# Feed-forward stage: rotation cosines read from PSUM, GELU table load moved, q/k norm by halves, order of the last DVE steps changed

## The reference

```python
h = shift_token(x)
q, k, v = split(h @ wqkv, 3)                    # 8 heads of 64
q, k = l2norm(q) * qs, l2norm(k) * ksc
q, k = rotary_xpos(q, k)                        # q*cos*scale + rotate_half(q)*sin*scale
o = local_attention(q, k, v)                    # band of 64, softmax
x = x + o @ wo
h = layernorm(shift_token(x)) * lg + lb
a, g = split(h @ w1 + b1, 2)
x = x + (a * gelu(g)) @ w2 + b2
```

## Time and profile before

| | |
|---|---|
| three executions | 2468.91, 2474.99, 2475.39 us; median 2474.99 |
| profiled execution | 2465.03 us, span 2462.9 us |
| mean granted clock of TensorE | 0.946 of full speed |
| busy: PE, DVE, ACT, POOL | 2116.9, 1809.3, 1462.6, 1058.3 us |

### The profile page before, as it was taken

One profiled execution on the slowest core, in us unless ns is written; L12 is line 12 of the kernel. 1 busy time (PEld: TensorE's weight loads), 2 busy tenths in 40 slices (PEclk: granted clock), 3 DMA queues, 4 the chain that ended last, 5 costly groups with the idle time before them and its releaser, 6 DMA issues. The chain is left out here.

```text
span 2462.9 us, 56322 instructions
## 1 busy us (share of the span) xinstructions
PE 2116.9 (86%) x23398; PEld 1565.7 (64%) x23398; DVE 1809.3 (73%) x2815; ACT 1462.6 (59%) x2389; POOL 1058.3 (43%) x800
## 2 busy tenths in 40 slices
PE   2799999998989868999868999999989997597968
PEld 1566666666666645555536667676666664495758
DVE  3688888888888646777727888888888884563556
ACT  0477776766666515666546776766666674363635
POOL 4665555545555210000035565655555450550245
PEclk8799999999999968999979999999999998698979
DMA  7000000079999995000000000000000003121122
GB/s 151 1 2 1 2 2 2 1 78 105 111 137 129 126 127 51 2 2 2 2 1 1 2 2 2 2 2 2 2 2 2 1 2 76 54 66 37 35 75 80
DMA packets 211376, 90.91 MB, mean 37 GB/s; under 512 B 79700, under 2 KB 206721, under 8 KB 210996
## 3 DMA queue, kind: packets, MB, share of 16 engines
q1 hardware_dynamic: 202596, 72.27, 24.5%
q0 software_dynamic: 6080, 11.76, 1.5%
q10 hardware_dynamic: 2448, 3.28, 0.6%
HBM read 24.31 MB, written 63.41 MB: 36 GB/s over the span
## 5 line engine op out<-in xcount | busy, mean ns | idle before, releaser
L490 POOL TENSOR_TENSOR work<-work,rot_tables 128x512 f32<-128x512 f32 x256 | 382.6, 1515 | 317.3 <-ACT work L594 317.3
L498 POOL TENSOR_TENSOR work<-work 128x1024 f32<-128x1024 f32 x128 | 304.8, 2381 | 283.6 <-DVE work L924 278.4
L941 DVE TENSOR_TENSOR work<-work,small 128x1024 f32<-128x1024 f32 x128 | 234.4, 1833 | 56.6 <-ACT small L608 50.1
L924 DVE TENSOR_TENSOR work<-work,rot_tables 128x1024 f32<-128x1024 f32 x128 | 219.3, 1713 | 11.6 <-ACT work L594 11.6
L1081 DVE TENSOR_REDUCE small<-psum 128x4 f32<-128x1024 f32 x128 | 156.6, 1223 | 90.3 <-PE psum L1582 88.5
L1482 PE MATMUL psum<-centered,ffn_w 128*128 128x256 f32 x768 | 191.2, 401 | 3.0 <-DVE centered L985 2.9
L705 ACT ACTIVATE work<-psum 128x1024 f32<-128x1024 f32 x128 | 131.0, 1024 | 88.7 <-PE psum L1582 88.4
L1323 PE MATMUL psum<-qkv_w_hi,h_hi 128*128 128x512 f32 x384 | 180.0, 469 | 2.2 <-ACT work L594 2.2
L1420 PE MATMUL psum<-work 64*128 64x128 f32 (+1 forms) x2048 | 178.9, 304 | 0.0
L1482 PEld LDWEIGHTS psum<-centered,ffn_w 128*128 128x128 f32 x768 | 146.0, 197 | 31.2 <-DVE centered L985 4.4
L1453 PE MATMUL psum<-work,v 128*32 128x192 f32 (+1 forms) x4096 | 164.8, 302 | 0.0
(11 more groups left out here) (279 smaller groups left out, 5266.1 us busy)
## 6 DMA issues: line engine op xcount, KB each, us to landing
h_area<-mean_weights SPq DMA_DIRECT2D x24, 2048.0 KB
tile_x<-h_area SPq DMA_DIRECT2D x39, 128.5 KB, 2.1
stage<-in_consts ACTq DMA_DIRECT2D x1, 2817.0 KB, 12.0
tile_x<-h_area SPq DMA_DIRECT2D x39, 64.5 KB, 1.8
work<-in_x SPq DMA_DIRECT2D x4, 512.0 KB, 27.2
expert_w<-in_ew SPq DMA_DIRECT2D x1, 2048.0 KB, 8.4
expert_w<-in_ew SPq DMA_DIRECT2D x8, 256.0 KB, 6.6
work<-y_tokens SPq DMA_DIRECT2D x4, 512.0 KB, 6.1
```

What stands on the lines that cost most here:

```text
L490: last = pool.tensor_tensor(b[:, :, :, o_], a[:, :, :, i_], tab[:, l, 1, t, :, o_].unsqueeze(2).to_broadcast([P, 2, HEADS, 32]), ALU.mult)
L498: pool.tensor_tensor(rC[:, t, :], rC[:, t, :], rB[:, t, :], ALU.add).then_inc(f_sum, 1)
L924: dve.tensor_tensor(g(rC[:, t, :]), g(rA[:, t, :]), tab[:, l, 0, t, :, :].unsqueeze(2).to_broadcast([P, 2, HEADS, DH]), ALU.mult)\
L941: dve.tensor_tensor(c_, c_, sm[0][:, 96 + 16 * t:112 + 16 * t].unsqueeze(2).to_broadcast([P, 16, DH]), ALU.mult).then_inc(f_nrm, 1)
```

## The change

- `cosines(i, t)` reads q and k from PSUM instead of from the SBUF copy, as soon as `qk(i, t)` is done. `copy_qk(i, t)` on ACT now waits until `cosines(i, t)` has read them.
- On DVE `cosines(i, 0)` moves up, ahead of `resid`, and `cosines(i, 1)` takes its old place.
- In `scores` the wait for `copy_qk(i, 0)` moves from the front to the third group of masks.
- On ACT the GELU table is asked for after `rstd`; `copy_v` comes ahead of `copy_qk(i, 1)`.
- `clip` and `rnorm` are done for each half t by itself. `rnorm(i, 0)` comes behind `gelu`, `rnorm(i, 1)` after two of the three `exps` and after `x_square`.
- On DVE the end of the turn becomes `gated`, `qk_norm(i, 0)`, `x_center`, `sums(i, 1)`, `clip(i, 1)`, `qk_norm(i, 1)`, `o_norm(i-1, 0)`, `resid2`. Before, it is `gated`, `sums(i, 1)`, `clip`, `x_center`, `qk_norm(i, 0)`, `resid2`, `qk_norm(i, 1)`, `o_norm(i-1, 0)`.
- `rotated` on POOL is two instructions of half the length. In `qk_T` all transposes of k come ahead of those of q. On PE `x_var` goes behind `attend(i-1, 1)`.

```diff
 MASKED = -1e30
 LN_SET = "natural_log_exp_and_others"
+GELU_SET = "gelu_and_others"
 
 
...
                     pool.wait_ge(f_sin, 2 * i + t + 1)
                     pool.wait_ge(f_cos, 2 * i + t + 1)
-                    pool.tensor_tensor(rC[:, t, :], rC[:, t, :], rB[:, t, :], ALU.add).then_inc(f_sum, 1)
+                    for h in range(2):
+                        n_ = slice(h * INNER, (h + 1) * INNER)
+                        last = pool.tensor_tensor(rC[:, t, n_], rC[:, t, n_], rB[:, t, n_], ALU.add)
+                    last.then_inc(f_sum, 1)
 
                 def normed(s):
...
             def ffn(f):
                 def copy_qk(i, t):
-                    act.wait_ge(f_qk, 3 * i + t + 1)
-                    free(act, f_cos, 2 * i + t - 1)
+                    act.wait_ge(f_cos, 2 * i + t + 1)
                     free(act, f_sin, 2 * i + t - 1)
                     src = PS[:, 1 + t:3 + t, :]
...
                     act.activation(V[i % 2][:, :, :], PS[:, 5:7, :], ACT.Copy).then_inc(f_vsb, 1)
 
-                def rnorm(i):
-                    act.wait_ge(f_ssm, i + 1)
-                    link(act.activation(sm[0][:, 64:96], sm[0][:, 32:64], ACT.Ln, scale=65536.0))
-                    act.activation(sm[0][:, 96:128], sm[0][:, 64:96], ACT.Exp, scale=-0.5, bias=half_ln[:, 0:1])\
-                        .then_inc(f_rn, 1)
+                def rnorm(i, t):
+                    part_ = lambda a: sm[0][:, a + 16 * t:a + 16 * t + 16]
+                    act.wait_ge(f_ssm, 2 * i + t + 1)
+                    link(act.activation(part_(64), part_(32), ACT.Ln, scale=65536.0))
+                    act.activation(part_(96), part_(64), ACT.Exp, scale=-0.5, bias=half_ln[:, 0:1]).then_inc(f_rn, 1)
 
                 def copy_q(i):
...
                         square(i - 2)
                         rstd(i - 2)
+                        act.preload_act_table_set(GELU_SET)
                     if new:
+                        copy_v(i)
                         copy_qk(i, 1)
-                        copy_v(i)
                         square_qk(i, 1)
                     if old:
                         gelu(i - 2)
+                    if new:
+                        rnorm(i, 0)
+                    if mid:
+                        exps(i - 1, 0)
+                        exps(i - 1, 1)
                     if pre:
                         x_square(n)
                     if new:
-                        rnorm(i)
+                        rnorm(i, 1)
                     if mid:
-                        for q in range(3):
-                            exps(i - 1, q)
+                        exps(i - 1, 2)
                     if mid:
                         recips(i - 1, 0)
...
                     l, _ = layer_of(i)
                     g = lambda x: x.rearrange("p (g h d) -> p g h d", g=2, h=HEADS)
-                    dve.wait_ge(f_cp, 2 * i + t + 1)
+                    dve.wait_ge(f_qk, 3 * i + t + 1)
                     free(dve, f_qT, i)
-                    dve.tensor_tensor(g(rC[:, t, :]), g(rA[:, t, :]),
+                    dve.tensor_tensor(g(rC[:, t, :]), PS[:, 1 + t:3 + t, :].rearrange("p g (h d) -> p g h d", h=HEADS),
                                       tab[:, l, 0, t, :, :].unsqueeze(2).to_broadcast([P, 2, HEADS, DH]), ALU.mult)\
                         .then_inc(f_cos, 1)
...
                 def sums(i, t):
                     dve.wait_ge(f_sq, 2 * i + t + 1)
-                    dve.tensor_reduce(sm[0][:, 16 * t:16 * t + 16], sq[:, t, :].rearrange("p (g d) -> p g d", d=DH), AX,
+                    dve.tensor_reduce(sm[0][:, 144 + 32 * t:176 + 32 * t:2], sq[:, t, :].rearrange("p (g d) -> p g d", d=DH), AX,
                                       ALU.add).then_inc(f_ss, 1)
 
-                def clip(i):
-                    dve.wait_ge(f_ss, 2 * i + 2)
-                    dve.tensor_scalar(sm[0][:, 32:64], sm[0][:, 0:32], 1e-24, None, ALU.max).then_inc(f_ssm, 1)
+                def clip(i, t):
+                    dve.wait_ge(f_ss, 2 * i + t + 1)
+                    dve.tensor_scalar(sm[0][:, 32 + 16 * t:48 + 16 * t], sm[0][:, 144 + 32 * t:176 + 32 * t:2], 1e-24, None, ALU.max)\
+                        .then_inc(f_ssm, 1)
 
                 def qk_norm(i, t):
-                    dve.wait_ge(f_rn, i + 1)
+                    dve.wait_ge(f_rn, 2 * i + t + 1)
                     dve.wait_ge(f_sum, 2 * i + t + 1)
                     c_ = rC[:, t, :].rearrange("p (g d) -> p g d", d=DH)
...
                     if mid:
                         k_out(i - 1)
+                    if new:
+                        cosines(i, 0)
                     if old:
                         resid(i - 2)
...
                         y_normed(i - 2)
                     if new:
-                        cosines(i, 0)
+                        cosines(i, 1)
                     if mid:
                         m_out(i - 1)
                     if new:
                         sums(i, 0)
-                        cosines(i, 1)
+                        clip(i, 0)
                     if old:
                         gated(i - 2)
                     if new:
-                        sums(i, 1)
-                        clip(i)
+                        qk_norm(i, 0)
                     if pre:
                         x_center(n)
                     if new:
-                        qk_norm(i, 0)
-                    if old:
-                        resid2(i - 2)
-                    if new:
+                        sums(i, 1)
+                        clip(i, 1)
                         qk_norm(i, 1)
                     if mid:
                         o_norm(i - 1, 0)
+                    if old:
+                        resid2(i - 2)
 
             def attn():
...
                         pe.wait_ge(f_nrm, 2 * i + t + 1)
                         last = turned(5, t, INNER)
-                        if t == TILES - 1:
-                            last.then_inc(f_kT, 1)
-                        else:
-                            free(pe, f_on, 2 * i - 1)
+                    last.then_inc(f_kT, 1)
+                    free(pe, f_on, 2 * i - 1)
+                    for t in range(TILES):
                         last = turned(3, t, 0)
                     last.then_inc(f_qT, 1)
...
                     pe.wait_ge(f_kb, i + 1)
                     pe.wait_ge(f_qsb, i + 1)
-                    pe.wait_ge(f_cp, min(2 * i + 3, 2 * ITEMS * (f + 1)))
                     groups = (((3, 6), range(8), P, 0, 0, ms0), ((4, 5), range(4), J0W, 1, WIN, ms1),
                               ((0, 1), range(4, 8), J0W, 1, WIN, ms1))
                     for bs, hs, w, _, _, m in groups:
+                        if bs[0] == 0:
+                            pe.wait_ge(f_cp, min(2 * i + 3, 2 * ITEMS * (f + 1)))
                         bands(bs, len(hs) // 2, w, m)
                     for bs, hs, w, t, k0, _ in groups:
...
                     if mid:
                         attend(i - 1, 0)
+                    if mid:
+                        attend(i - 1, 1)
                     if pre:
                         x_var(n)
-                    if mid:
-                        attend(i - 1, 1)
 
             def attn():
```

## The result

The changed kernel takes 2578.6 us (median of 4, 2572.9 to 2580.7). The kernel before beside it takes 2472.0 (4 runs). The ratio is 1.0436, 95% interval 1.0416 to 1.0456: slower by 107 us, where 93 were forecast. Its profiled execution has a span of 2576.0.

What follows compares the result with a forecast made beforehand. No engine was full, so a chain through several engines was taken to set the pace. Per call 12 x 2.5 + 4 x 0.85 + 14 x 0.8 = 44.6, plus 2; two calls 93; 2475 + 93 = 2568 us, range 2500 to 2620.

Steps and rivals of the forecast that it cites:

- The products wait for the copy: On PE, all products stand behind masks waiting for copy_qk, itself behind cosines; 0.7 us per turn without pre.
- slack before GELU: Earlier rotated(i, 0) may hold m_split and y_normed up to 0.4 per turn, counted as nothing; 24 us without slack.
- S: The start of the first s_max, from which the forecast counts the steps of a turn in us.
- The third `exps` behind `rnorm(i, 1)`: On ACT, the third exps queues behind the later rnorm(i, 1), so attend(i-1, 1) starts at 15.95, not 15.5; 0.1 per turn.
- DVE behind it: DVE's steps from exps through cosines(i+1, 0) fit ahead of resid, possible at 22.25 against 22.16; next s_max at 24.0.
- The turns with a layer 1 item: Feed-forward turns with a layer 1 old item, 14 per call, go from 24.09 to 24.9, +0.8.
- `qk_norm(i, 0)` held by POOL: On DVE, qk_norm(i, 0) could start at 11.3 but ends at 13.15, 1.1 after POOL's rotated; 12.5 if not held.
- The turns with `pre`: Late x_center delays down, and x_rstd delays recips on ACT; 12 turns per call go from 24.24 to 26.7, +2.5.
- Rival (2): Only the terms without pre are real, as x_rstd ends inside attend's time; +50, 2525 us; chance 0.17.
- rival (3): Losses of turns with pre and gains of the others cancel; 2470 to 2480 us; chance 0.04.
- the rival of two more: On ACT, square_qk needs its own table set, adding two loads per turn; +154 on top of 93, 2722 us; chance 0.05.
- Rival (1): Faster: DVE's own list sets the pace and the added waits are covered; 2343 us, or 2410; chance 0.10.

Runs made afterwards that it cites:

- c1b_cos: Kernel before with only the PSUM cosines, their new DVE places, copy_qk waiting for them and copy_v ahead of copy_qk(i, 1); scores wait at the front; ratio 1.0182.
- e1_masks: Changed kernel with the products of the first two groups ahead of the wait for the copy and the third group's masks; ratio 1.0343 to the kernel before.
- e4_sums: Changed kernel with sums and clip of both halves ahead of gated, and rnorm of both ahead of all exps; ratio 1.0244 to the kernel before.
- e5b_xvar_resid2: Changed kernel with x_var back between the two attends and resid2 back ahead of qk_norm(i, 1); ratio 1.0124 to the kernel before.
- e3_xcenter: Changed kernel with x_center back ahead of qk_norm(i, 0); ratio 1.0342 to the kernel before.
- e2_xvar: Changed kernel with x_var back between the two halves of attend; ratio 1.0395 to the kernel before.
- e6b_masks_pool: e1_masks with one more wait on POOL, meant to keep rotated(i, 0) from starting before m_split; ratio 1.0360 to the kernel before.
- g1b_gelu: Kernel before with only the GELU table asked for behind rstd; ratio 1.0004.
- best3b: Changed kernel with the edits of e1_masks, e3_xcenter, e4_sums and e5b_xvar_resid2, plus the POOL wait of e6b_masks_pool; 2412.6 us, ratio 0.9747 to the kernel before.
- best4b: best3b with gated ahead of sums(i, 1) and clip(i, 1); ratio 0.9946 to the kernel before.

## Why the prediction was right, step by step

The sign, the size and the length of each kind of turn were right. Not all of the terms behind them were.

**The products wait for the copy.** Forecast 0.7; the wait ahead of `s_max` is 0.73. As a wait it was right, and as a difference too: from `resid` to `s_max` it is 494.78 - 493.19 = 1.59 in the next turn, where it was 1.00 before. c1b_cos, which has this wait and not the new norm, is 1.06 longer in these turns. But it isn't what one gets back by removing it: without it (e1_masks) a turn is 0.24 shorter. The step that failed is the one that put `m_split` and `y_normed` at nothing, "slack before GELU". That slack was there only because the products were late; take the wait away and POOL's hold takes its place. A sum over the path can't tell that two terms lie beside each other. The same step had a slip of its own. It put `rotated(i, 0)` at 3.6 to 6.0 behind S; by the forecast's own terms (copy done 0.7 ahead of S, then 2.5 of `sines`) it runs from 1.8 to 4.2. The first row of POOL below has it at 1.89 to 4.42 in the turn shown, so that `m_split` stands inside its second half. From `s_max` to the end of `m_split` that costs 0.78 (4.69 against 3.91), about twice the 0.4 that the forecast allowed:

```profile
472.63 2.53 POOL L501 TENSOR_TENSOR work<-work 128x512 f32<-128x512 f32 x2
...
480.61 2.50 POOL L501 TENSOR_TENSOR work<-work 128x512 f32<-128x512 f32 x2
```

**The third `exps` behind `rnorm(i, 1)`.** Forecast 0.1 for the late `attend`. As a difference to the kernel before it is 0.3: `resid` comes at 22.45 behind S, before at 22.16. As what the order costs it is 0.9 to 1.1 per turn without `pre`, by e4_sums. The step compared with the kernel before, where `attend` was nearly as late for another reason, and never asked what the 1.45 gained at `qk_norm(i, 0)` would be worth without the hold (it ends at 482.04 + 2.15 - 470.74 = 13.45, before at 14.9). It is the term that was mis-sized.

**DVE behind it.** `resid` at S + 22.25 by the forecast, 493.19 - 470.74 = 22.45 measured; S again at 24.0 by the forecast, 24.04 measured.

**The turns with a layer 1 item.** Forecast +0.8, measured +0.82, and the match is largely luck. The forecast let the 0.85 of `resid2`'s second step cancel ("which before is as much longer") and gave the whole to `attend` and the copy. But c1b_cos, which has the copy's wait, makes these turns only 0.16 longer (24.25 against 24.09), where the forecast had 0.7 for it. The rest comes with the new order, and either of two edits undoes the whole: these turns have no `x_var`, so in e5b_xvar_resid2 only the place of `resid2` changes in them, and they take 23.99, while `s_max` still waits 0.48 for the products; with e4_sums and `resid2` late they take 23.82. So these two losses aren't a sum.

**`qk_norm(i, 0)` held by POOL.** Forecast at 11.3 and ending at 13.15; it starts 482.04 - 470.74 = 11.30 behind S and ends at 13.45, as `rotated` in two halves takes 2.50 and not 2.35 (the second row above). This is also the 0.3 by which the turns with `pre` are longer than forecast: `x_center` and `down` follow it, and in the turn with `pre` shown above `down` starts 13.98 behind S, against 13.65 forecast; every later step of the chain is as late. The rule cited for it, from the Trainium skill, SBUF — State Buffer, section "SBUF: two separate sides", agrees with these rows: DVE arrived in the second half and got nothing from the split.

**The turns with `pre`.** Forecast +2.5, measured +2.82. The two mechanisms are the ones named, `x_center` ahead of `down` (1.70 of wait) and `x_rstd` ahead of `recips` (2.60 of wait). e3_xcenter gives 0.41 for the first by itself. For the second the forecast named half of the cause. It took `x_var`'s place; e2_xvar shows that this place alone can't be taken back, because `x_var` then waits for `resid2`, and e5b_xvar_resid2 that the two together can, for 1.55 per turn. Rival (2), that `x_rstd` would end inside `attend`'s time, fell by the same rows, and rival (3), no change, by the time alone.

**Four turns of 28.70.** Not in the sum. In them the granted clock fell behind `down`'s wait. The profile's windows over the 5.4 us after that pause, in one such turn and in the next, of 27.06 (columns: window, its length, busy time and instructions of each engine, granted clock, DMA share and GB/s):

```profile
132.60:138.00 5.40, 5.35 (x74) 3.83 (x78) 2.78 (x4) 2.38 (x6) 0.55 (x1) 0.68 0.00 0
161.30:166.70 5.40, 5.19 (x103) 4.16 (x104) 3.99 (x6) 2.26 (x6) 0.63 (x1) 1.00 0.01 3
```

The timeline of PE has `down` in both:

```profile
132.65 2.48 PE L1503 MATMUL psum<-gated,ffn_w 128*128 128x256 f32 x6 [1.70 <-DVE centered L1022]
...
161.34 1.53 PE L1503 MATMUL psum<-gated,ffn_w 128*128 128x256 f32 x6 [1.70 <-DVE centered L1022]
```

The clock is 0.68 of full speed in the one, which is part of it at 1.2 GHz, and 1.00 in the other, behind the same pause of 1.70. The slow turns cost 1.65 each, about 6.6 us. The forecast had a lower clock only as a bound, at 25. The runs together say more than this kernel alone. Five kernels have the pause of 1.70 in all their 24 turns with `pre` (the first turn of each call left out), and the clock fell in four of them here, five in e1_masks, none in e2_xvar, four in e5b_xvar_resid2 and eight in e6b_masks_pool. In the other nine the pause is 1.47 or less, and it fell in none of their turns with `pre`, e3_xcenter among them. So no such loss is seen without the pause, but the pause alone isn't enough for it. In e3_xcenter it fell once elsewhere, in a turn with a layer 1 item of 27.38, behind 2.17 us of idle PE that no engine's wait explains.

**What went at nothing and did.** The GELU table (g1b_gelu, 1.0004): ACT has no gap between `rstd` and GELU, so an earlier load moves nothing. In the changed kernel, too, a turn has two loads (L673 and L648), as its timeline of ACT shows, so the rival of two more fell:

```profile
474.66 1.28 ACT L673 ACT_TABLE_LOAD   x1
475.96 1.02 ACT L606 ACTIVATE v<-psum 128x1024 f32<-128x1024 f32 x1
476.93 1.02 ACT L597 ACTIVATE work<-psum 128x1024 f32<-128x1024 f32 x1
477.99 1.06 ACT L602 ACTIVATE qk_squares<-work 128x1024 f32<-128x1024 f32 x1
478.95 1.19 ACT L646 ACTIVATE gelu<-psum,b 128x256 f32<-128x256 f32 x3
480.15 1.28 ACT L648 ACT_TABLE_LOAD   x1
```

The Trainium skill, ScalarE: Activation LUTs, section "Table sets: the hidden batching unit", doesn't list square; these rows show a square and two copies under the GELU set with no load of their own.

**Rival (1), DVE's own list.** It fell for this change: DVE's list didn't get the 2.2 us shorter. Its busy time in a turn without `pre` is 20.45, where it was 20.30. The 1.22 of `cosines(i, 0)` moved into the gap, and the stretch that `cosines(i, 1)` and `qk_norm(i, 0)` lost came back on the cast in `m_split` and on `clip(i, 0)`, 0.95 each in place of 0.18. But its condition, that `qk_norm(i, 1)` be over by 15 after S, is close to what best3b reaches, 454.31 + 1.23 - 439.33 = 16.2 by the rows of best3b, and with it turns of 22.7.

**Sum.** The forecast by kinds was 12 x 2.5 + 4 x 0.85 + 14 x 0.8 = 44.6 per call and 2 for the ends. Measured: 12 x 2.82 + 3.3 (clock) + 3.4 + 14 x 0.82 = 52. What it was short of is 0.3 x 24 and the clock's 6.6. The totals, 93 and 107, don't show that the +0.8 with a layer 1 item had for the most part another cause than the one named.

What stays open: why the clock falls in four of 24 like turns and not in the others, and never in e2_xvar; what `resid2` back by itself would give; whether `y_normed` can be put ahead of `rotated` in e6b_masks_pool by waiting for `y_normed` itself, which wasn't tried; and what is next in best3b, where the first `s_max` follows `resid` at once and PE waits 1.09 for `gated`.

## What to carry to other kernels

Moving work into a gap helps only if nobody behind it in the chain waits for what the moved work holds: here `cosines` filled DVE's idle 1.6 us and held a copy, four masks and with them all products. When a step moves down an engine's list (`resid2`), look for who shares its bank or its semaphore; the cost appeared on two other engines. Parts that lose together can win apart from their neighbours: five small changes of order turned 1.044 into 0.981, and one wait more into 0.975, with the PSUM read (and the order on ACT that comes with it) worth 1.0% of it.

## What the runs showed of the hardware that I hadn't expected

A very small DVE instruction can be held as long as a large one. Beside a POOL instruction of 1.26, `clip` on 16 columns takes up to 1.20 (best4b) where it takes 0.17 alone, the cast in `m_split` on 32 columns 0.95 to 1.04 (changed kernel) in place of 0.18, and its subtraction 1.21 (e1_masks) in place of 0.19. Which of the two engines goes first is decided within 0.01 us in e6b_masks_pool: `y_normed` was held in every turn in which `rotated` started 6 ns or more ahead of it, and in none with 4 ns or less. The outcome can be the same for most turns of a loop, so one loop can have turns of 24.24 and 24.78 with no difference in the program.
